# A graph layer's merge: the words that name each step's chunk, kept as 16-bit in place of 32-bit words

## What is computed

```python
def _egnn_conv(x, src, dst, edge_attr, W_msg, W_edge, W_root, b):
    msg = x[src] @ W_msg + edge_attr @ W_edge
    agg = jax.ops.segment_max(msg, dst, num_segments=x.shape[0])
    agg = jnp.where(jnp.isneginf(agg), 0.0, agg)
    return agg + x @ W_root + b
c1 = jax.nn.leaky_relu(_egnn_conv(X, src, dst, edge_attr, W1_msg, W1_edge, W1_root, b1))
c2 = jax.nn.leaky_relu(_egnn_conv(c1, src, dst, edge_attr, W2_msg, W2_edge, W2_root, b2))
# result: _layernorm(x + c2)
```

## Time and profile before

| | us |
|---|---|
| median of 3 runs | 2114.91 (2101.77 to 2116.11) |
| span of the profiled execution | 1855.9 |
| PE busy | 1587.7 (86%) |
| DVE busy | 1330.7 (72%) |
| ACT busy | 1159.0 (62%) |
| POOL busy | 1082.9 (58%) |
| HBM read and written | 264 MB and 173 MB |

### The profile page before, as it was taken

How to read it: one execution, slowest core, us unless ns; L and a number is a source line. 1 busy time by engine, 2 the same in 40 slices (tenths; PEclk the granted TensorE clock), 3 DMA queues, 4 the chain that set the end, 5 groups by cost and what they waited for, 6 DMA issues and landing times.

```text
span 1855.9 us, 38086 instructions
## 1 busy us (share of the span) xinstructions
PE 1587.7 (86%) x11618; PEld 1353.7 (73%) x11618; DVE 1330.7 (72%) x2383; ACT 1159.0 (62%) x2646; POOL 1082.9 (58%) x1454
## 2 busy tenths in 40 slices
PE   3999999999989888886999999999987767676663
PEld 2767877877778888885787777777777666666663
DVE  2667777777765555554677777777736899999998
ACT  2455555656533455563566666666636788888887
POOL 6767777777700000003777777777757778765753
PEclk9999999999999999998999999999999999888887
DMA  6769999999955778885777777777767899999996
GB/s 124 190 163 257 278 265 251 266 276 252 254 190 187 230 252 268 275 280 156 198 215 213 209 215 205 216 212 209 213 213 220 272 297 302 295 299 299 299 296 177
DMA packets 558474, 440.19 MB, mean 237 GB/s; under 512 B 445619, under 2 KB 465786, under 8 KB 558282
## 3 DMA queue, kind: packets, MB, share of 16 engines
q1 hardware_dynamic: 476396, 282.87, 53.3%
q10 hardware_dynamic: 50910, 97.16, 14.3%
q0 software_dynamic: 30976, 57.72, 14.0%
HBM read 264.25 MB, written 173.37 MB: 236 GB/s over the span
## 4 chain that ended last, share of the span: by engine, by line
PE 43%; DVE 21%; POOL 15%; DMA 10%; issue 9%; ACT 1%; SPq 1%; ACTq 0%; DVEq 0%; POOLq 0%
PE ps L561 18%; POOL arena L385 13%; PE ps L472 9%; DMA onehot_bytes<-keep 7%; DVE stats L942 6%; PE ps L463 5%; PE ps L441 4%; DVE arena L940 4%; DVE arena L937 4%; PE ps L430 2%; DVE keep L885 2%; POOL onehot L417 2%; DMA arena<-nodes,src_perm 2%; PE ps L451 2%; PE ps L435 2%
## 5 line engine op out<-in xcount | busy, mean ns | idle before, releaser
L561 PE MATMUL ps<-hold,onehot 128*128 x4688 | 614.1, 293 | 182.7 <-POOL onehot L417 131.8
L561 PEld LDWEIGHTS ps<-hold,onehot 128*128 128x128 f32 x4688 | 583.2, 205 | 213.8 <-issue 213.4
L385 POOL DMA_INDIRECT arena<-nodes,src_perm x392 | 369.9, 944 | 469.8 <-SPq L352 350.7
L472 PEld LDWEIGHTS ps<-w_root,onehot 97*128 97x128 f32 x3136 | 397.0, 192 | 96.6 <-issue 95.9
L385 POOL DMA_INDIRECT arena<-in_x_dram,src_all x392 | 376.4, 960 | 128.4 <-issue 114.6
L472 PE MATMUL ps<-w_root,onehot 97*128 97x128 f32 x3136 | 414.3, 275 | 0.0
L417 POOL CAST onehot<-keep 128x256 f32<-128x256 uint8 x588 | 294.9, 550 | 115.4 <-PE ps L561 57.7
L871 DVE TENSOR_TENSOR_SCAN arena<-keep,arena,ps 96x512 f32<-96x512 bf16 x196 | 248.3, 1267 | 71.3 <-PE ps L441 68.3
L689 ACT COPY arena<-ps 128x384 f32<-128x384 f32 x392 | 166.6, 476 | 210.7 <-PE ps L561 210.6
L629 ACT COPY arena<-ps 128x384 f32<-128x384 f32 x392 | 190.5, 486 | 159.1 <-PE ps L472 158.2
L885 DVE TENSOR_TENSOR onehot<-count,rel 128x1024 f32<-128x1024 bf16 x147 | 179.6, 1222 | 143.8 <-PE ps L561 139.2
(11 more groups left out here) (100 smaller groups left out, 1401.7 us busy)
## 6 DMA issues: line engine op xcount, KB each, us to landing
root<-arena ACTq DMA_DIRECT2D x196, 384.0 KB
arena<-root SPq DMA_DIRECT2D x196, 384.0 KB, 4.6
nodes<-arena SPq DMA_DIRECT2D x98, 384.0 KB, 2.7
arena<-nodes SPq DMA_DIRECT2D x98, 384.0 KB
arena<-in_x_dram SPq DMA_DIRECT2D x97, 384.0 KB
arena<-in_x_dram SPq DMA_DIRECT2D x48, 768.0 KB, 8.1
out_dram<-arena SPq DMA_DIRECT2D x48, 768.0 KB, 4.7
onehot_bytes<-keep ACTq DMA_DIRECT2D x147, 128.0 KB
```

The costliest lines, as they stand in the source:

```text
L385: nc.gpsimd.indirect_dma_start(out=gathered[t.ring][0:t.p, i, 0:D], out_offset=None, in_=table_in, in_offset=bass.IndirectOffsetOnAxis(ap= ...
L472: last = nc.tensor.matmul(no_ps[m % 2][:, i * P:(i + 1) * P], nodes_t[m % NODE_RING][0:D + 1, i * P:(i + 1) * P], w_root[0:D + 1, layer * ...
L561: nc.tensor.matmul(ps_bytes[:, bass.ds(place_at, SLOT)].bitcast(F32), onehot[:, k % NS, i, :], flat[:, bass.ds(chunk_at, P)], start=False, ...
```

## The change

The row of step words is seen as unsigned 16-bit in place of signed 32-bit: `step_words` covers the first 588 32-bit words of the row, read as 1176 halves. VectorE's instruction in `piece_words` converts to that type, and `load_words` reads 16 halves in place of 16 words; its registers, their count and all that follows are written as before. The largest word is 390 x 96 = 37440, below 65536.

```diff
+U16 = mybir.dt.uint16
...
+    assert TP % 2 == 0 and CH * D < 1 << 16
...
-        step_words, ones_row = rows[0:1, :], ones_all[ROWS_ON:, :]
+        step_words, ones_row = rows[0:1, 0:TP // 2].bitcast(U16), ones_all[ROWS_ON:, :]
```

## The result

The changed kernel takes 2446.65 us (median of 4 runs, 2443.26 to 2454.0) against 2114.38 before: ratio 1.161, interval 1.157 to 1.165. The forecast was 2068 us. The kernel became 332 us slower; the rival "halves are read one by one" had 2400.

The account below looks back on a forecast made before the run. TensorE's sequencer was taken to bound merge 0. Shorter loads would save 49 us there, less 5 for transfers (-44), and 3 in merge 1: -47 us, forecast 2068 us, range 2050 to 2114.

Parts of the forecast that it names:

- halves are read one by one: Rival: each 16-bit half fetched singly, 4.35 us a load; merge 0 +217, merge 1 +68, 2400 us; chance 0.11.
- What bounds merge 0: Merge 0: TensorE's sequencer is the bound, 3.0 us plus the load, with the array 0.5 to 0.8 us behind.
- spacing = 3.0 us + the load: Merge 0, time between loads: 3.0 + 0.57 plus 0.14 disturbance, 3.71 us in place of 4.38.
- The queue of 64 instructions: TensorE: queue ahead of the array would hide the load, no change, 2115 us; rival hidden or given back, chance 0.03.
- The price of a load: TensorE's loads in the merges: 16 bytes a fetch, so 32 bytes take 0.57 us in place of 1.10; chance 0.60.
- 184: TensorE's loads, 16 words against 8: 184 ns, 23 a register; supports rival priced by register, 2115 us, chance 0.10.
- the sum on transfers: Late merge 0: DMA engines would pace, 80 us x 0.86 / 0.97 = 71 in place of 68; 5 us taken off.
- the 259 us between span and median: Whole kernel: median 2114.9 lies 259 us above the profiled span 1855.9, taken as the same time around it in both.

Follow-up runs that it names:

- Experiments 7 and 8: Both against the kernel before: 32-bit words in bytes, one multiplication fewer a step, 2095.9 us; two such words a step, twice the loads, 2130.0 us.
- the packed kernel: Changed kernel with its 16-bit words loaded as 32-bit pairs, split by a mask or shift each step: 2214.7 us, ratio 1.0515 against the kernel before.
- experiment 3: Kernel before with its row of 32-bit words moved by one word (4 bytes): 2451.7 us, ratio 1.164.
- experiment 1: Kernel before, unchanged, profiled a second time: 2100.5 us in one run, span 2098.6.

## Why the prediction was wrong

**What bounds merge 0: right.** The sequencer's register work and load set the pace. Its model (spacing = 3.0 us + the load) gives 3.0 + 4.33 = 7.3 us for the changed kernel and 7.61 was measured; a third of the rest is that the loads' mean, 4.44 us in the trace, is above their median. Experiments 7 and 8 follow from it too. The queue of 64 instructions that the Trainium skill's page "TensorE: Matmul & The Clock Gate" gives (table at the head) hid no part of the longer loads in merge 0: spacing grew by 3.18 us, the loads' median by 3.03.

**The price of a load: right for words, wrong for halves.** This is the step that failed: "32 bytes make 0.30 + 0.27 = 0.57 us ... since the equality of one word and four has no other simple reading". For whole words the sizes were right, and nothing speaks against the reading. Undisturbed, 4, 8 and 16 whole words take 331, 587 and 1101 ns: 74 ns and 257 for each 16 bytes. (The 331 is the packed kernel's last load of layer 0, shown below.) What failed is the step from bytes to elements. The rows of before bore out grouping for 32-bit words that follow each other from such starts, and for nothing else; I carried it over to 16-bit elements with "nothing shows that it needs 32-bit words", which was as true of its opposite. Each 16-bit element costs a fetch of its own, 232.5 ns, as each 32-bit word does in a row that starts 4 bytes off (experiment 3). The load measured 3782 ns undisturbed and 4334 at the median, not 570.

```profile
L548 PEldq TENSOR_LOAD <-rows x2: 331/754/1177, 1076.5 to 1082.7; - x2
```

**Two small slips.** The rows give 1101 - 921 = 180 ns between 16 words and 8, not 184. And the 0.97 in the sum on transfers stands in no row; with the 0.99 of the earlier trace rows the 71 us would be 69.5. Neither moves the forecast by more than 2 us.

**The slow rival: right in mechanism, a little off in sizes.** It priced an element at 0.27, it measured 0.232, so 16 take 3.78 us in place of 4.35. But the disturbance is larger, too: it adds 0.55 at the median, where it added 0.16 to 0.2, and brings the load to 4.33, almost what the rival had. Merge 0 was to lose 217 us and lost 233 (563 against 330). Merge 1 was to lose 68 and lost 108: the rival took the sequencer's undisturbed 7.35 us against 6.4, and 7.96 was measured, with loads up to 6 us in that stage. Together 341 in place of 285, and 2447 in place of 2400.

**The chances.** A slow path at 0.11 against 0.60 for the fetch of 16 bytes was the real error. There was no row of a 16-bit load, by the prediction's own sums the price of the slow path (285 us) was six times the gain of the fast one (47), and nothing in the trace spoke on which held. The range left it out.

**The transfers.** They were never put to the test, since no version brought the spacing near 3.7 us. The forecast of the DMA engines as the next bound stays unproven.

**The profile's own time.** Nearly all of the 259 us between span and median were in the edge phases (experiment 1); the sum did not depend on it.

## What to carry to other kernels

A load into registers by TensorE's sequencer has two speeds here. Keep the words in 32 bits and start each load where these fast ones started, at multiples of 32 bytes (16 was enough for ScalarE's four words); then 16 bytes cost about 257 ns. The same count of 16-bit elements took half the bytes and over three times the time. Where the sequencer sets the pace, price a step by its instructions: ten nanoseconds less inside a fused register instruction came out at the end, and one more instruction of 36 ns beside it cost 140. When a resource's fast path was seen only under certain conditions, give the case outside these conditions a large chance and keep it in the range.

## What the runs showed of the hardware

- Loads by TensorE's sequencer, undisturbed: 331, 587, 1101 ns for 4, 8, 16 whole words from a start at a multiple of 32 bytes in the tile; 1922 and 3782 ns for 8 and 16 halves; 1934 and 3797 ns for 8 and 16 whole words from a row that starts 4 bytes off. The prices are about 257 ns for 16 bytes, or 233 ns for each element.
- Loads get longer by disturbance: those of 3782 ns at the least took up to 7932 in layer 0 of the changed kernel and up to 6059 in layer 1, those of 1101 up to 3275 in merge 0 of the second profile. What disturbs them stayed open; no run took it apart.
- Where the matmul array waits some microseconds in every pair of batches, the mean granted clock was 0.84 in merge 0 in place of 0.99, with stretches at 1.2 GHz, and 359 us busy for what took 283. The pace there, set by the sequencer, hardly changed by it.
- A wait that the profile puts down to another engine can be a sequencer's load: 48 us named for one-hots were the load's.
- In one profiled execution of the unchanged kernel both edge phases were 117 and 130 us shorter than in the second profile of the same kernel, with a higher granted clock and a higher share of the DMA engines; no other profile had them so short. What made them so is open.
